# Self attention of a decoder layer: seven shared value blocks for two batches, and another order in two batches

## What is computed

```python
qkv = x @ w_qkv
q, k, v = jnp.split(qkv, 3, axis=-1)
sim = jnp.einsum('bhid,bhjd->bhij', q, k) * scale
attn = jax.nn.softmax(sim, axis=-1)
out = jnp.einsum('bhij,bhjd->bhid', attn, v)
return out @ w_out + b_out
...
x = _layernorm(x + _L0_attn_ref(x, w_qkv, w_out, b_out), axis=-1)
```

## Time and profile before

| | |
|---|---|
| median of 3 runs | 427.19 us (427.08 to 427.41) |
| the profiled execution | 428.63 us |
| its span, first to last instruction | 426.9 us |
| PE busy | 402.9 us, 94% of the span |
| PE weight loads | 284.7 us, 67% |
| DVE busy | 252.5 us, 59% |
| ACT busy | 192.5 us, 45% |
| GpSimd busy | 51.2 us, 12% |
| mean granted clock of PE | 0.992 |
| self attention | 22 to 161 us of the span |

### The profile page before, as it was taken

One profiled execution on the slowest core, in us unless ns is written; L12 is line 12 of the kernel. 1 busy time (PEld: TensorE's weight loads), 2 busy tenths in 40 slices (PEclk: granted clock), 3 DMA queues, 4 the chain that ended last, 5 costly groups with the idle time before them and its releaser, 6 DMA issues.

```text
span 426.9 us, 12682 instructions
## 1 busy us (share of the span) xinstructions
PE 402.9 (94%) x4986; PEld 284.7 (67%) x4987; DVE 252.5 (59%) x729; ACT 192.5 (45%) x575; POOL 51.2 (12%) x79
## 2 busy tenths in 40 slices
PE   8989999999999788999999999999899999999992
PEld 7857878878787565666666666666565475566661
DVE  1357775856667555666668676768673642244443
ACT  1054462443616526677667656667683101111220
POOL 4010001101011001000001010100100054222333
PEclk9999999999999999999999999999999999999998
DMA  7998100000000013050404040920000013121210
GB/s 250 381 390 239 33 3 3 2 5 2 4 3 2 4 38 134 16 185 3 185 2 185 9 178 2 374 110 2 0 4 2 2 61 100 62 62 58 71 44 25
DMA packets 15255, 34.48 MB, mean 81 GB/s; under 512 B 2381, under 2 KB 9150, under 8 KB 13920
## 3 DMA queue, kind: packets, MB, share of 16 engines
q1 hardware_dynamic: 13952, 30.72, 20.5%
q0 software_dynamic: 1104, 2.76, 1.8%
q10 hardware_dynamic: 144, 0.23, 0.2%
HBM read 27.27 MB, written 6.70 MB: 80 GB/s over the span
## 4 chain that ended last, share of the span: by engine, by line
PE 47%; issue 38%; DVE 9%; ACT 4%; POOL 2%; POOLq 0%; DVEq 0%; ACTq 0%
PE banks L444 9%; PE banks L830 5%; PE banks L923 4%; PE banks L899 4%; PE banks L905 4%; PE banks L466 4%; PE banks L521 3%; PE banks L486 3%; ACT p L984 3%; PE banks L842 3%; PE banks L508 3%; DVE p L1155 2%; DVE pT L1164 1%; DVE nm L1147 1%; POOL xb L377 1%
## 5 line engine op out<-in xcount | busy, mean ns | idle before, releaser
L1285 DVE CUSTOM_DVE_ANT_0 p<-banks,mask 112x375 f32<-112x375 f32 x128 | 62.6, 542 | 28.2 <-PE banks L633 28.1
L1038 ACT ACTIVATE p<-p,nm 112x375 f32<-112x375 f32 x128 | 73.8, 603 | 5.3 <-DVE nm L1285 5.2
L1045 ACT ACTIVATE pT<-banks 128x336 f32<-128x336 f32 x96 | 42.3, 442 | 42.2 <-PE banks L653 41.9
L653 PEld LDWEIGHTS banks<-ident,p 112*128 112x128 f32 (+1 forms) x384 | 38.4, 140 | 28.9 <-issue 22.0
L984 ACT ACTIVATE p<-banks,nm 128x112 f32<-128x112 f32 x128 | 43.2, 363 | 31.5 <-DVE nm L1147 31.5
L653 PE MATMUL banks<-ident,p 112*128 112x112 f32 (+1 forms) x384 | 53.2, 266 | 1.9 <-DVE nm L1285 1.5
L444 PE MATMUL banks<-x2T,arena 128*128 128x224 f32 x256 | 52.5, 361 | 0.0
L444 PEld LDWEIGHTS banks<-x2T,arena 128*128 128x128 f32 x256 | 48.9, 194 | 1.8 <-ACT arena L974 0.2
L359 POOL TENSOR_TENSOR rstd<-veps,minus_half 128x1 f32<-128x1 f32 x14 | 7.7, 551 | 286.1 <-DVE veps L1179 286.1
L1140 DVE TENSOR_SCALAR arena<-banks 128x448 f32<-128x448 f32 x32 | 19.8, 620 | 28.9 <-PE banks L444 28.9
L466 PE MATMUL banks<-arena,x2T 128*32 128x256 f32 (+1 forms) x512 | 29.9, 381 | 1.7 <-issue 1.4
(11 more groups left out here) (144 smaller groups left out, 566.8 us busy)
## 6 DMA issues: line engine op xcount, KB each, us to landing
arena<-in_ug SPq DMA_DIRECT2D x8, 1024.0 KB, 5.7
arena<-in_dn SPq DMA_DIRECT2D x8, 512.0 KB, 6.7
mid<-in_ctxT SPq DMA_DIRECT2D x8, 375.0 KB, 3.3
slots_s<-blank SPq DMA_DIRECT2D x14, 128.5 KB
arena<-in_wqk SPq DMA_DIRECT2D x7, 256.0 KB, 6.1
slots_x<-blank SPq DMA_DIRECT2D x14, 128.0 KB
p<-slots_s SPq DMA_DIRECT2D x9, 128.5 KB, 2.0
kT<-slots_x SPq DMA_DIRECT2D x9, 128.0 KB, 2.1
```

Of the source, the lines that this page charges most:

```text
L653: mm = pe.transpose(PE_T2[r][0:k1 - k0, t * S:(t + 1) * S], p2_rows[:, i % RING, k0:k1], ident[0:S, 0:S])
L1038: act.activation(p2[i % RING], p2[i % RING], ACT.Exp, bias=nm2[:, i % H:i % H + 1], scale=-1.0).then_inc(exp2, 1)
L1045: act.activation(pT2[:, i % RING], PE_T2[r][:, 0:KT * S].rearrange("p (k n) -> p k n", k=KT), ACT.Copy).then_inc(pt2_act, 1)
L1285: v.tensor_tensor_reduce(p2[i % RING], PE_S2[r][0:S, 0:S2], bias[:], 1.0, 3e38, ALU.add, ALU.min, accum_out=nm2[:, i % H:i % H + 1]).then_ ...
```

## The change

Two batches (224 tokens) are seven blocks of 32. The even batch projects four blocks, the last of which holds its own last 16 tokens and the first 16 of the odd batch; the odd batch projects only the three that are left (`project_v1`). `v1_block` names where a batch's block lies; the shared block is kept in the last place of `v1[0]` or `v1[1]`, and ACT drains an odd batch's second half as one block, and an even batch's in one or two instructions. For an odd batch the probability rows must then begin 16 columns into their first block, so a row of `p1` gets 16 zero columns on either side of its 112, and the transpose reads 128 columns starting at the left pad (odd) or at the first probability (even). GpSimd zeroes both pads. The values of an odd batch contract over all 32 rows of each block, those of an even one over 16 in its last.

In batches 2 and 4 (`early`), `out1(b - 2)` stands ahead of the scores of pair 1 instead of behind, and the values of pair 1 stand behind between 5. On DVE one drain moves ahead of the third normalise and one ahead of the fourth, and `ln1_a` goes from ahead of the fourth normalise to behind the fourth transpose. The waits inside `value1`, `out1` and `score1` are as they were.

```diff
@@ -142,8 +142,10 @@
         bias = mask0
 
 
-        p1_all = p2_all[:, 0:4 * QB * 128].rearrange("p (g i n) -> p g i n", g=4, i=QB)
-        p1 = [p1_all[:, g] for g in range(4)]
+        PAD = QB * SQ - S
+        p1_all = p2_all[:, 0:4 * QB * (S + 2 * PAD)].rearrange("p (g i n) -> p g i n", g=4, i=QB)
+        p1 = [p1_all[:, g, :, PAD:PAD + S] for g in range(4)]
+        p1_blocks = [[p1_all[:, g, :, (1 - odd) * PAD:(1 - odd) * PAD + QB * SQ] for g in range(4)] for odd in range(2)]
         pT1 = [pT_all[:, g * QB * 128:(g + 1) * QB * 128].rearrange("p (j n) -> p j n", j=QB) for g in range(4)]
         SH = 4 * TILE
         hTs = pT_all[:, 0:HT * SH].rearrange("p (k n) -> p k n", k=HT)
@@ -238,6 +240,14 @@
         PE_T2 = (bank[4], bank[7], PE_S2[0], PE_S2[1])
         PE_L2 = PE_S2[2]
 
+        def v1_block(b, j):
+
+            if b % 2 == 0 and j < QB - 1:
+                return v1[0][:, j]
+            if b % 2 == 1 and j > 0:
+                return v1[1][:, j - 1]
+            return v1[b // 2 % 2][:, QB - 1]
+
         def block1(j, full=True):
 
             return SQ if full or (j + 1) * SQ <= S else S - j * SQ
@@ -337,9 +347,10 @@
                             pattern=[[-1, 128]], channel_multiplier=1).then_inc(consts, 1)
             g.wait_ge(consts, 4)
             g.memset(ones[:], 1.0).then_inc(consts, 1)
-            g.memset(p1_all[:, :, :, S:128], 0.0).then_inc(padded1, 1)
+            g.memset(p1_all[:, :, :, 0:PAD], 0.0).then_inc(padded1, 1)
+            g.memset(p1_all[:, :, :, PAD + S:], 0.0).then_inc(padded1, 1)
             g.memset(v2_all[:], 0.0).then_inc(v2_ones, 1)
-            g.wait_ge(padded1, 1)
+            g.wait_ge(padded1, 2)
             g.memset(p2_rows[:, :, S2:SP], 0.0).then_inc(p2_padded, 1)
             g.wait_ge(v2_ones, 1)
             g.memset(v2[:, :, :, :, D2:D2 + 1], 1.0).then_inc(v2_ones, 1)
@@ -458,13 +469,13 @@
                     pe.wait_ge(qk_sb, 4 * b + 3 + c)
                 if (b, c) == (3, 0):
                     pe.wait_ge(prep, 7)
-                for j in (2 * c, 2 * c + 1):
-                    m = block1(j, b % 2 == 0)
-                    at = (b % 2) * S + j * SQ
+                odd = b % 2
+                for n in range(1 if odd and c else 2):
+                    at = (odd * QB + 2 * c + n) * SQ
                     for k in range(KC):
                         for strip in range(STRIPS):
-                            mm = pe.matmul(PE_J1[c][SQ * strip:SQ * strip + m, (j % 2) * 256:(j % 2) * 256 + 256],
-                                           xT[:, b // 2, k, at:at + m], wv1[:, strip // 2, k, (strip % 2) * 256:(strip % 2) * 256 + 256],
+                            mm = pe.matmul(PE_J1[c][SQ * strip:SQ * strip + SQ, n * 256:n * 256 + 256],
+                                           xT[:, b // 2, k, at:at + SQ], wv1[:, strip // 2, k, (strip % 2) * 256:(strip % 2) * 256 + 256],
                                            start=(k == 0), stop=(k == KC - 1))
                 mm.then_inc(v1_pe, 1)
 
@@ -500,13 +511,13 @@
                 if b >= 2:
                     pe.wait_ge(y1, b - 1)
                 for j in range(QB):
-                    n = block1(j, False)
+                    n = block1(j, b % 2 == 1)
                     for par in range(2):
                         at = (2 * pair + par) * D1
                         for strip in range(STRIPS):
                             rows_s = slice(SQ * strip, SQ * strip + n)
                             mm = pe.matmul(PE_U1[strip][64 * par:64 * par + 64, pair * S:(pair + 1) * S],
-                                           v1[b % 2][rows_s, j, at:at + D1], pT1[2 * pair + par][rows_s, j, 0:S],
+                                           v1_block(b, j)[rows_s, at:at + D1], pT1[2 * pair + par][rows_s, j, 0:S],
                                            start=(j == 0), stop=(j == QB - 1))
                 mm.then_inc(pv1[pair], 1)
 
@@ -590,23 +601,26 @@
             for c in range(2):
                 project_v1(0, c)
             for b in range(B):
+                early = b in (2, 4)
                 score1(0, b)
                 between1(b, 0)
                 between1(b, 1)
+                if early:
+                    out1(b - 2)
                 score1(1, b)
-                if b >= 2:
+                if b >= 2 and not early:
                     out1(b - 2)
                 between1(b, 2)
                 between1(b, 3)
                 if b < B - 1:
                     value1(0, b)
-                if 2 <= b < B - 1:
+                if 2 <= b < B - 1 and not early:
                     value1(1, b)
                 between1(b, 4)
                 between1(b, 5)
                 if b == B - 1:
                     value1(0, b)
-                if b < 2 or b == B - 1:
+                if b < 2 or early or b == B - 1:
                     value1(1, b)
                 if b == 1:
                     pe.wait_ge(prep, 5)
@@ -971,7 +985,13 @@
                 act.wait_ge(v1_pe, 2 * b + c + 1)
                 if b >= 2:
                     act.wait_ge(pv1[1], b - 1)
-                act.activation(v1[b % 2][:, 2 * c:2 * c + 2].rearrange("p j n -> p (j n)"), PE_J1[c][:, :], ACT.Copy).then_inc(v1_sb, 1)
+                if c == 0 or b % 4 == 0:
+                    act.activation(v1[b % 2][:, 2 * c:2 * c + 2].rearrange("p j n -> p (j n)"), PE_J1[c][:, :], ACT.Copy).then_inc(v1_sb, 1)
+                elif b % 2 == 1:
+                    act.activation(v1[1][:, 2], PE_J1[c][:, 0:256], ACT.Copy).then_inc(v1_sb, 1)
+                else:
+                    act.activation(v1[0][:, 2], PE_J1[c][:, 0:256], ACT.Copy)
+                    act.activation(v1[1][:, 3], PE_J1[c][:, 256:512], ACT.Copy).then_inc(v1_sb, 1)
 
             def exps(g, b):
                 if (g, b) == (0, 0):
@@ -981,7 +1001,7 @@
                     act.wait_ge(turned1, b * 4 + (g - 3))
                 for i in range(QB):
                     n = QB * g + i
-                    e = act.activation(p1[g][:, i, 0:S], PE_S1[g % 2][:, i * 128:i * 128 + S], ACT.Exp,
+                    e = act.activation(p1[g][:, i], PE_S1[g % 2][:, i * 128:i * 128 + S], ACT.Exp,
                                        bias=nm1[:, n:n + 1], accum_out=rs1[:, n:n + 1])
                 e.then_inc(exp1[g], 1)
 
@@ -1152,7 +1172,7 @@
                 v.wait_ge(exp1[g], b + 1)
                 v.reciprocal(rc1[:, c], rs1[:, c]).then_inc(rcp1, 1)
                 v.wait_ge(rcp1, b * 4 + (g + 1))
-                v.tensor_tensor(p1[g][:, :, 0:S], p1[g][:, :, 0:S], rc1[:, c].unsqueeze(2).to_broadcast([128, QB, S]), ALU.mult).then_inc(norm1, 1)
+                v.tensor_tensor(p1[g], p1[g], rc1[:, c].unsqueeze(2).to_broadcast([128, QB, S]), ALU.mult).then_inc(norm1, 1)
 
             def turn_blocks(g, b):
 
@@ -1160,9 +1180,9 @@
                 if b >= 1:
                     v.wait_ge(pv1[g // 2], b)
                 elif g == 0:
-                    v.wait_ge(padded1, 1)
+                    v.wait_ge(padded1, 2)
                 v.transpose(pT1[g].rearrange("p j (i a) -> p i j a", i=QB),
-                            p1[g].rearrange("p i (j a) -> p i j a", j=QB)).then_inc(turned1, 1)
+                            p1_blocks[b % 2][g].rearrange("p i (j a) -> p i j a", j=QB)).then_inc(turned1, 1)
 
             def add_rest(src, done, added, b, p, sy):
                 v.wait_ge(done, b + 1)
@@ -1254,19 +1274,23 @@
                 turn_blocks(1, b)
                 rowmax(2, b)
                 rowmax(3, b)
-                if b < 2:
+                early = b in (2, 4)
+                if b < 2 or early:
                     drain1(b, 0)
                 normalise(2, b)
                 turn_blocks(2, b)
-                if b >= 2:
+                if b >= 2 and not early:
                     ln1_a(b - 2)
                     drain1(b, 0)
                 else:
                     drain1(b, 1)
                 normalise(3, b)
                 turn_blocks(3, b)
+                if early:
+                    ln1_a(b - 2)
                 if b >= 2:
                     ln1_b(b - 2)
+                if b >= 2 and not early:
                     drain1(b, 1)
                 drain1(b, 2)
                 drain1(b, 3)
```

## The result

The changed kernel takes 434.54 us as the median of 4 runs (434.07 to 436.69); the kernel before took 427.19 in the same series. The ratio is 1.0173, with a 95% interval of 1.0145 to 1.0200. So the change costs 7 to 10 us (9.0 by the second ratio, 9.9 by its medians). I had forecast 432.0 with a range up to 434.2: the right way and the right place, but too little.

A forecast was written before the change was run, and what follows sets the result against it. TensorE (PE), busy 94% of the span, was taken to bound the kernel. Batches 0, 2, 4 and 6 gave -0.91 + 2.15 + 1.88 + 0.0 = +3.1 us; with 1.7 for one clock fall, 427.19 became 432.0 us, range 429.0 to 434.2.

The forecast's parts named there:

- The bound, and the wait: Batches 2 and 4: PE, the engine that bounds, would idle 3.09 us before the values of pair 0, waiting for y1.
- Batches 2 and 4 without the clock: Batch 2 would last 20.30 us against 18.15 (+2.15), batch 4 19.98 against 18.10 (+1.88), at an unchanged clock.
- Batch 6, batches 3 and 5: Batch 6 stays 15.8 us, with 0.9 us idle before scores of pair 1; batches 3 and 5 at 18.1.
- Batch 0: Its projection drops one of four blocks: -0.91 us, or a gain of 0 to 2.3 if the issue hole moves.
- one fall is the likeliest: Clock drops to 1.2 GHz behind one of the two new idles, costing 1.69 us: 432.0 us; chance 0.42.
- The rival of two falls: Clock drops behind both new idles, in batches 2 and 4, 3.4 us more: 433.7 us; chance 0.22.
- The range: Whole kernel, 429.0 to 434.2 us: no, one or two clock falls, with the bounds of the idle.
- its bound for the idle: PE's idle before the values of pair 0 in batches 2 and 4: 2.3 to 3.6 us around 3.09.
- the rivals as I had them: No fall 430.3 us (0.28), two falls 433.7 (0.22), y1 not last 424.1 (0.05), cost cancels savings 427.2 (0.03).
- The median and the profiled execution: Whole kernel: +3.1 us added to the runs' median, 427.19; the profiled execution's 428.63 lies 1.44 us above it.

The follow-up runs named there:

- e4: Changed kernel with only the residual add that raises y1 put ahead of the row maxima of groups 2 and 3 in batches 2 and 4: 424.23 us, ratio 0.9923.
- e2: Kernel before with only the new order in batches 2 and 4, four blocks for every batch: 436.71 us against 427.43, ratio 1.0212.
- e6: Changed kernel with three dead matmuls on PE ahead of the wait of the values of pair 0 in batches 2 and 4: 432.78 us, ratio 1.0131.
- e1: Seven blocks and padded rows alone, batches 2 and 4 in the order of the kernel before: 426.88 us against 427.43, ratio 0.9991.
- e8: The changed kernel itself, run again in a second series on one chip: 436.88 us against 426.96, ratio 1.0211.
- e9: Kernel before with the 28 DMAs that zero the slot tables held back until the values of batch 1 are done: 427.24 us against 427.46, ratio 1.0002.
- e10: e1 with the 28 DMAs that zero the slot tables held back until the values of batch 1 are done: 427.08 us against 427.46, ratio 0.9990.
- e3: Changed kernel with six dead matmuls on PE ahead of the wait of the values of pair 0 in batches 2 and 4: 431.27 us, ratio 1.0095.

## Why the prediction was wrong

*The bound, and the wait.* That y1 would be last at the values of pair 0, for 3.09 us, was right: 3.09 and 3.08 us. Taking the offsets of batch 0, the one place in the trace with the new DVE order, worked to 0.1 us. e4 shows by removal that the wait is the cause, e2 that the blocks have no part in it.

*Batches 2 and 4 without the clock.* Forecast 20.30 and 19.98 us; 20.48 and 20.10 in e6. Together 0.3 us too little.

*Batch 6, batches 3 and 5.* Forecast unchanged, with 0.9 us of idle in batch 6: batches 3 and 5 last 18.09 us each, batch 6 15.84 with 0.90 of idle, and e1 shows the same idle in batch 4 when the order is left alone.

*Batch 0.* Forecast -0.91; measured -0.37 (15.78 against 16.15, from 22.02 to 38.17). The range that I gave for it, 0 to 2.3, held it. The term counted PE work and assumed that the holes stay what they are. Up to the scores of pair 1 the batch did gain 0.84 us; the new hole took 0.47 back (from the values of pair 0 to the next projection 1.53 us instead of 1.06).

*The clock, where it failed.* The step "one fall is the likeliest", at 1.69 us each, was wrong twice. Dense projections beside the idle protect nothing: both idles had their fall in both profiles of the changed kernel and in e2's. And one row was no price: in these batches a fall costs 1.5 to 2.8 us, and in batch 7, where the row stands, the batch as a whole lost 1.35. With 4.3 us of longer batches, 0.4 gained and two falls, the sum is 7.2 us at the price of the first profile and 9.5 at e8's, and the medians say 7.35 and 9.9. The rival of two falls had 0.22 and stood at 433.7, still below the result, since it used the same single price.

*The range.* It had no bound for the price of a fall, and its bound for the idle was added once though there are two idles. With 0.5 us more for each (3.6 instead of 3.09) the upper end is 434.7 us, and with 0.8 less for each the lower end is 428.7. So even the rivals as I had them reached past 434.2; but e8's 436.88 lies beyond 434.7 too, and there the longer falls make the difference.

The Trainium skill ("TensorE: Matmul & The Clock Gate", section "HAM oscillation") says that waits that recur in a loop bring the lower clock back each time. Its case is a short loop, and the two idles here stand 40 us apart, so to apply it was a stretch of mine. The trace of the changed kernel agrees, with two falls for two new idles; e9 and e10, with an idle of 3.03 us and no fall, show that it isn't so every time.

*The median and the profiled execution.* I added the change to the median of the runs and left 1.44 us between it and the profiled execution unexplained. The fall in batch 7 is 1.35 us, which the profiled run (mean clock 0.992) had and, by their clocks, some ordinary runs hadn't. That fits; the clocks of the three runs behind the first median aren't on record. Two profiles have no fall there (e9, e10; below e9's), and the idle of 3.03 us passes at the upper clock:

```profile
145.61 1.07 PE L487 MATMUL banks<-arena 64*32 64x112 f32 x64 [3.03 <-ACT p L985]
146.61 3.72 PE L522 MATMUL banks<-arena 128*128 128x256 f32 x16
```

## What to carry to other kernels

When work moves, look at which semaphore each moved instruction raises, and who waits for it, however small the instruction: here the 0.39 us add was the first thing in a moved group, and its waiter had been left where it stood. Split such a group, and keep ahead what others wait for. Price an idle of PE with what the clock does behind it, from both sides, and where an idle can't be removed, dead matmuls inside it are worth trying: 2.75 us of them in each of two idles gave 3.3 us back. And look at the mean granted clock of each run before comparing medians: here it told runs with one fall more from those without, where the medians mixed them.

## What the runs showed of the hardware

Of 16 idles of 3.0 to 3.1 us in ten profiles, the granted clock went to 0.5 behind or at the end of 14, with dense projections before them in batches 2 and 4 and scores and transposes in batch 7; of four idles of 0.5 to 1.8 us in batches 2 and 4 (e3, e6) behind none. The two without a fall are both in batch 7, in e9 and e10. In e4 a hole of 1.71 us in batch 0 did have one:

```profile
33.20 0.93 PE L519 MATMUL banks<-pT,arena 32*64 32x112 f32 x48 [1.71 <-issue]
34.07 4.98 PE L455 MATMUL banks<-x2T,arena 128*128 128x224 f32 x16
...
36.00:37.00 1.00, 1.00 (x5) 0.50 0.40 126
```

so a short idle is no warrant either. I had not expected the clock to fall so regularly behind an idle that lies between dense work.
